# Two token tiles to a PSUM bank for the transposes of the exponentials and of the queries

## The chip, the cores and the metric

The kernel runs on one core of one Trainium2 chip, as one program. The metric is device time in microseconds from the first to the last instruction of one execution, with what the runtime adds around it. TensorE (PE) multiplies and transposes into PSUM; ScalarE (ACT) and VectorE (DVE) read PSUM and write SBUF; GpSimd (POOL) issues the gathers; SyncE (SP) issues the other transfers. Each engine runs its own stream in order, and the streams meet in semaphores.

## The reference, cut to what matters

A graph of 3125 nodes with 256 features and 100000 edges goes through one layer. Three things are added to the input: a graph convolution over the edges, four layers of linear attention with feed-forward blocks, and a mixture of 16 experts with two chosen per node. The change lies in the linear attention:

```python
def _linear_attn(x, Wq, Wk, Wv, Wo, bo):           # 8 heads of 32
    split = lambda t: t.reshape(b, n, HEADS, DH).transpose(0, 2, 1, 3)
    scale = DH ** (-0.25)
    q = jax.nn.softmax(split(x @ Wq) * scale, axis=-1)   # over a head's 32 columns
    k = jax.nn.softmax(split(x @ Wk) * scale, axis=-2)   # over all 3125 tokens
    v = split(x @ Wv)
    context = jnp.einsum('bhnd,bhne->bhde', k, v)
    out = jnp.einsum('bhnd,bhde->bhne', q, context)
    return out.transpose(0, 2, 1, 3).reshape(b, n, dm) @ Wo + bo

def _forward(x, ...):
    for i in range(4):
        x = x + _linear_attn(_layernorm(x, ln1_g[i], ln1_b[i]), ...)
        h = _layernorm(x, ln2_g[i], ln2_b[i])
        x = x + (jax.nn.gelu(h @ W1[i] + b1[i], approximate=False) @ W2[i] + b2[i])
    return x
```

## The kernel before, in words

**Tiles.** The 3125 tokens are 25 tiles of T = 125 tokens; five tiles (GT) are a group, and there are five groups (NG). 256 features are KD = 2 halves of 128. Pieces PC split a group in 3 and 2 tiles; units RP split it in 2, 1 and 2 tiles (NRP = 3 units).

**PSUM.** Eight banks of 512 fp32 columns. Two take edge products (`edge_bank`), one the sums over edges (`sum_bank`), two are the `ROW` pair that VectorE empties, and three (banks 4, 6, 7) are the ring, which ScalarE empties. Everything that TensorE puts into the ring is a numbered unit u; it goes to `RING[(u - RING_A) % 3]`. TensorE asks for a unit with `ring(u)` (line 1229), which waits until unit u - 3 has been copied out (`ring_act`), and reports it with `ring_full`. The numbers are laid out by hand in lines 348 to 406: `RING_GA` units per group in the key stage, `RING_MP` between, `RING_GP` per group in the feed-forward stage. The order in which TensorE fills units and ScalarE empties them must be the same.

**Key stage, per layer.** For each group g: TensorE waits until all earlier units are copied (line 1301), makes the keys, transposed, as four units (line 1310); VectorE takes the maximum over the tokens (1760) and from it a bias; ScalarE writes the exponentials `eT` (1012), features in partitions, tokens in columns. Meanwhile the next group's normalised tokens are transposed (1255) and scaled to `TT` or `TTQ` by ScalarE (`features`, 939). Then the exponentials are transposed back to tokens in partitions (1321 to 1327): one unit per token tile, two transposes of 128 columns each, and `copy_tile` (942 to 944, called at 1023 to 1025) copies each unit to `es[:, j, :]`, 125x256. The product of `es` with the normalised tokens is the context (`context`, 1287 to 1297), one group late; after the last group at once.

**Queries.** Query rows come from `Wq_s` through the `ROW` pair; VectorE and ScalarE make the softmax in `qe` (tokens in partitions). `queries_T` (TensorE 1266 to 1272, ScalarE 997 to 1000) transposes `qe` tile by tile: one unit per token tile, two transposes, one copy of 128x250 to `QT`. `attention(g, units)` (1277 to 1280) multiplies `QT` with `M_s`, unit by unit of RP, and waits at line 1279 until all tiles of the unit are copied. Group 0's queries are transposed between key and feed-forward stage, those of group g + 1 after the first half of the feed-forward block of group g (1380 to 1384).

**Edge steps.** The graph convolution's 224 edge steps are strewn by hand between all this (`step`): TensorE multiplies edge attributes (437) and sums rows by destination (429, 430), VectorE adds gathered rows (`z`, 477), ScalarE takes the positive part (`zr`, 445), VectorE the low part (`zl`, 451), GpSimd gathers the next rows (875). In ScalarE's stream an edge step stands right ahead of the copies of `es` in groups 0 to 3 (line 1022) and ahead of the copies of `QT` in groups 1 to 4 (line 1057); in the last key group the queries of group 0 stand there for TensorE (1318 to 1320).

**Graph stage, after the layers.** `pairs_T` (TensorE 1398 to 1405, ScalarE 1075 to 1080) already transposes by units of two, one and two tiles, with copies of 128x500 and 128x250.

Of the kernel before, what the change touches and what calls it, by code (L numbers as in the profile page):

```python
# [11 lines left out]
def build(nc, x, src, dst, edge_attr, gnn_W1, gnn_b1, gnn_W2,  # L12
# [56 lines left out]
    with ExitStack() as ctx:  # L69
# [12 lines left out]
        def sem(name):  # L82
# [235 lines left out]
        l_init, k_max, m_new, nb_done, cd_done, m_cp, corr_done = (sem(n) for n in (  # L318
            "l_init", "k_max", "m_new", "nb_done", "cd_done", "m_cp", "corr_done"))
# [29 lines left out]
        RING_GA = [4 + (LNU if g + 1 < NG else 0) + GT for g in range(NG)]  # L349
        RP = ((0, 2), (2, 3), (3, 5))  # L350
        NRP = len(RP)
        pair_of = lambda j: next(i for i, (a, b) in enumerate(RP) if a <= j < b)
        ROW_GA = 2
        RING_GP = [2 * NF + (GT + LNU if g + 1 < NG else 0) for g in range(NG)]
        QIN = [1 <= g < NG - 1 for g in range(NG)]
        ROW_GP = [NRP * (1 + (g + 1 < NG) + QIN[g]) for g in range(NG)]
        RING_MP, ROW_MP = 1 + GT + LNU, 3 * NRP + 1 + KD
# [46 lines left out]
        def ring_h2(l, g):  # L404
            return ring_qT(l, g) + GT
# [511 lines left out]
        def _(act):  # L917
# [56 lines left out]
            for l in range(L):  # L974
# [22 lines left out]
                def queries_T(g):  # L997
                    u = ring_qT(l, g)
                    for j in range(GT):
                        copy_tile(u + j, u + j - RING_A, QT[:, :, j * T:(j + 1) * T], T)  # L1000
# [5 lines left out]
                for g in range(NG):  # L1006
# [16 lines left out]
                    for j in range(GT):  # L1023
                        u = ring_k(l, g + 1) - GT + j
                        copy_tile(u, u - RING_A, es[:, j, :].rearrange("p (k n) -> p k n", k=KD), 128, T)
# [113 lines left out]
        def _(pe):  # L1139
# [119 lines left out]
            for l in range(L):  # L1259
# [6 lines left out]
                def queries_T(g):  # L1266
                    pe.wait_ge(q_norm, l * NG + g + 1)
                    for j in range(GT):
                        to = ring(ring_qT(l, g) + j)
                        for k in range(KD):  # L1270
                            ins = pe.transpose(to[:, 128 * k:128 * k + T], qe[:, j, 128 * k:128 * k + 128], ident[0:T, 0:T])
                        ins.then_inc(ring_full, 1)
# [4 lines left out]
                def attention(g, units):  # L1277
                    for i in units:
                        pe.wait_ge(ring_act, ring_qT(l, g) + RP[i][1] + 1)
                        rows_at(row_ao(l, g), i, lambda j: [(QT[:, k, j * T:(j + 1) * T], M_s[:, k, :]) for k in range(KD)])  # L1280
# [6 lines left out]
                def context(g):  # L1287
                    r0, uT = row_c(l, g), ring_k(l, g + 1) - GT
                    for pc, (a, b) in enumerate(PC):
                        to = row_of(r0 + pc)  # L1290
                        for h in range(KD):
                            for j in range(a, b):
                                if h == 0:
                                    pe.wait_ge(ring_act, uT + j + 2)
                                ins = pe.matmul(to[:, D * h:D * h + D], es[:, j, 128 * h:128 * h + 128], NORM[g % 2][:, j, :],  # L1295
                                                start=j == a, stop=j == b - 1)
                        ins.then_inc(row_full, 1)

                for g in range(NG):
                    u0, uT = ring_k(l, g), ring_k(l, g + 1) - GT  # L1300
# [20 lines left out]
                    for pc, (a, b) in enumerate(PC):  # L1321
                        for j in range(a, b):
                            pe.wait_ge(ring_act, u0 + (2 * pc + 3))
                            to = ring(uT + j)
                            for h in range(KD):
                                ins = pe.transpose(to[0:T, 128 * h:128 * h + 128], eT[:, h, j * T:(j + 1) * T], ident[:, :])
                            ins.then_inc(ring_full, 1)
# [715 lines left out]
```

## Time and profile before

| what | value |
|---|---|
| time, median of 3 runs | 2347.41 us (2334.14 to 2352.9) |
| the profiled execution: time | 2339.37 us |
| the profiled execution: span | 2337.6 us |
| mean granted TensorE clock | 0.935 of 2.4 GHz |
| busy: PE, PEld, DVE, ACT, POOL | 84%, 68%, 63%, 39%, 58% of the span |
| chain that ended last, by engine | PE 54%, DVE 18%, DMA 9%, ACT 7%, issue 6%, POOL 3% |

PE is TensorE's matrix work, PEld its weight loads, which overlap it. Busy time is a mean over stages with different limits; the chain is the work that released the next work, followed back from the last instruction, and tells which engine the end hung on at each moment. Its shares are of the whole span, the edge set-up before 180 us, four layers until about 1850 us, the graph stage and the experts included. Matmuls are pipelined, so the ends of PE pieces are modelled.

### The profile page before, as it was taken

The page shows a single profiled execution, that of the slowest core. Times are in us where ns is not written, and L with a number is a line of the kernel's source. Part 1 is how long each engine was busy: PE and PEld are TensorE (multiplying, and loading weights), DVE is VectorE, ACT ScalarE, POOL GpSimd, SP SyncE. Part 2 cuts the span into 40 slices and gives each one's busy share as a digit, 9 for nine tenths or more (in the row PEclk, how much of TensorE's full clock was granted, in tenths as well). Part 3 has the DMA queues.
Part 4 walks back from the last instruction along what each step waited for, and adds up shares of the span by engine and source line. Part 5 has one row for each costly group of instructions (what it writes and reads, how often), then busy time and mean ns, then how long its engine had stood idle before and what let it go on. Part 6 is the DMA issues. An engine that isn't in the chain of part 4 may idle for free.

```text
span 2337.6 us, 31898 instructions
## 1 busy us (share of the span) xinstructions
PE 1962.4 (84%) x10094; PEld 1594.8 (68%) x10094; DVE 1463.9 (63%) x3291; ACT 910.5 (39%) x1964; POOL 1356.0 (58%) x1123
## 2 busy tenths in 40 slices
PE   2448889999888999988899999889999985899990
PEld 1326667778666777866678777668777775788880
DVE  4747686766778677676876777686666557311116
ACT  1224344443435444344444444444444231233330
POOL 4157386667647666775666667567666500566650
PEclk9759999999999999999999999999999986899995
DMA  8564243333533332353333335343333421899997
GB/s 213 177 169 114 76 103 85 83 72 81 148 102 96 86 81 73 80 154 103 90 88 86 73 73 145 106 107 93 77 78 76 117 77 44 261 304 302 301 269 169
DMA packets 275536, 294.06 MB, mean 126 GB/s; under 512 B 146715, under 2 KB 204126, under 8 KB 275390
## 3 DMA queue, kind: packets, MB, share of 16 engines
q0 software_dynamic: 127488, 134.76, 24.0%
q1 hardware_dynamic: 143790, 157.50, 22.6%
q8 instruction: 70, 1.15, 0.2%
q10 hardware_dynamic: 4112, 0.03, 0.1%
q14 instruction: 76, 0.62, 0.1%
HBM read 243.19 MB, written 47.87 MB: 125 GB/s over the span
## 4 chain that ended last, share of the span: by engine, by line
PE 54%; DVE 18%; DMA 9%; ACT 7%; issue 6%; POOL 3%; SPq 1%; DVEq 1%; POOLq 0%; ACTq 0%
PE bank L1245 23%; PE bank L1373 11%; DMA TTQ<-zn_d,slot_tok 3%; PE bank L429 3%; PE bank L430 3%; PE bank L437 3%; DVE zl L451 2%; PE bank L1485 2%; DVE z L477 2%; DMA aT<-attr_d 2%; PE bank L1493 2%; ACT zr L445 2%; PE bank L1295 2%; POOL G L875 1%; PE bank L1310 1%
## 5 line engine op out<-in xcount | busy, mean ns | idle before, releaser
L875 POOL DMA_INDIRECT G<-P_d,src_T x896 | 1134.0, 1266 | 649.8 <-DVE z L477 382.6
L445 ACT ACTIVATE zr<-z 125x512 fp32r<-125x512 f32 x448 | 266.9, 629 | 349.2 <-DVE z L477 305.6
L451 DVE SCALAR_TENSOR_TENSOR zl<-z,zr 125x512 fp32r<-125x512 f32 x448 | 289.9, 688 | 140.3 <-ACT zr L445 130.9
L477 DVE TENSOR_TENSOR z<-bank,G 125x512 f32<-125x512 f32 x448 | 289.4, 684 | 136.7 <-PE bank L437 68.1
L1373 PE MATMUL bank<-TT,W_s 128*128 128x250 f32 (+1 forms) x1280 | 361.6, 428 | 15.9 <-ACT hid L1054 15.9
L1245 PE MATMUL bank<-W_s,hid 128*125 128x256 f32 x1600 | 361.1, 379 | 2.2 <-ACT hid L1054 2.2
L1245 PEld LDWEIGHTS bank<-W_s,hid 128*125 128x125 f32 x1600 | 293.8, 188 | 46.0 <-ACT hid L1054 3.8
L1373 PEld LDWEIGHTS bank<-TT,W_s 128*128 128x128 f32 x1280 | 235.7, 190 | 112.4 <-ACT hid L1054 23.1
L429 PE MATMUL bank<-zr,onehot 125*125 125x256 f32 x896 | 269.2, 332 | 21.8 <-DVE zl L451 21.7
L1054 ACT ACTIVATE hid<-bank,b_s 128x375 f32<-128x375 f32 x320 | 163.3, 521 | 271.3 <-PE bank L1373 223.6
L430 PE MATMUL bank<-zl,onehot 125*125 125x256 f32 x896 | 229.2, 286 | 0.0
L429 PEld LDWEIGHTS bank<-zr,onehot 125*125 125x125 f32 x896 | 170.9, 191 | 48.3 <-DVE onehot L464 30.1
L437 PE MATMUL bank<-Wst,aT 128*125 128x512 bf16 x448 | 139.2, 390 | 60.4 <-DMA aT<-attr_d 54.3
L430 PEld LDWEIGHTS bank<-zl,onehot 125*125 125x125 f32 x896 | 171.9, 192 | 5.6
L464 DVE TENSOR_TENSOR onehot<-iota_n,dst_T 125x500 fp32r<-125x500 f32 x224 | 152.5, 681 | 0.0
L1688 DVE TENSOR_TENSOR X<-bank,X 125x512 f32<-125x512 f32 (+1 forms) x120 | 71.5, 598 | 107.3 <-PE bank L1245 94.6
L437 PEld LDWEIGHTS bank<-Wst,aT 128*125 128x125 bf16 x448 | 59.4, 139 | 93.4 <-issue 49.4
L939 ACT ACTIVATE TT<-bank,lnp 128x250 f32<-128x250 f32 (+1 forms) x128 | 67.9, 613 | 114.8 <-PE bank L1255 109.9
L1119 ACT ACTIVATE QT<-bank,b1e 128x128 f32<-128x128 f32 x256 | 73.2, 369 | 98.8 <-PE bank L1485 76.3
L895 POOL DMA_INDIRECT TTQ<-zn_d,slot_tok x32 | 31.5, 986 | 137.9 <-DVE slot_tok L1971 121.3
L1245 PE MATMUL bank<-M_s,QT 128*125 128x256 f32 x400 | 104.9, 414 | 2.1 <-DVE M_s L1793 2.1
L1245 PE MATMUL bank<-Wq_s,TTQ 128*125 128x256 f32 x400 | 96.2, 381 | 5.8 <-DVE qe L1671 5.8
(317 smaller groups left out, 2953.1 us busy)
## 6 DMA issues: line engine op xcount, KB each, us to landing
W_s<-in_L_ffn_w SPq DMA_DIRECT2D x64, 512.0 KB
hid<-in_L_ffn_w SPq DMA_DIRECT2D x64, 512.0 KB
G<-P_d,src_T POOLq DMA_INDIRECT x896
TTQ<-nT_d SPq DMA_DIRECT2D x20, 626.0 KB
W_s<-in_L_mix_W SPq DMA_DIRECT2D x8, 1024.0 KB
nT_d<-TT SPq DMA_DIRECT2D x12, 626.0 KB
aT<-attr_d SPq DMA_DIRECT2D x224, 31.2 KB
nT_d<-TTQ SPq DMA_DIRECT2D x8, 626.0 KB
```

Source lines behind the costliest of these rows:

```text
L429: nc.tensor.matmul(sum_bank[0:T, 0:D], onehot[:, s, i, :], zr[:, s, i // 2, cols], start=i == 0, stop=False)
L430: ins = nc.tensor.matmul(sum_bank[0:T, 0:D], onehot[:, s, i, :], zl[:, i // 2, cols], start=False, stop=i == ST - 1)
L437: nc.tensor.matmul(edge_bank[k][0:ET, :], aT[:, s, :], Wst[:, 2 * k * D:2 * (k + 1) * D], start=True, stop=True).then_inc(e_done, 1)
L445: nc.scalar.activation(zr[:, s, k, :], z[:, k, :], ACT.Relu).then_inc(r_done, 1)
L451: nc.vector.scalar_tensor_tensor(zl[:, k, :], z[:, k, :], 0.0, zr[:, s, k, :].bitcast(f32), ALU.max, ALU.subtract).then_inc(lo_done, 1)
L464: nc.vector.tensor_tensor(onehot[:, s, :, :], iota_n[0:ET, :].unsqueeze(1).to_broadcast([ET, ST, T]), dst_T[:, ds(e * ST, ST)].unsqueeze(2 ...
L477: nc.vector.tensor_tensor(z[:, k, :], edge_bank[k][0:ET, :], G[:, ST * s + 2 * k:ST * s + 2 * k + 2, :].rearrange("p j d -> p (j d)"), ALU ...
L875: pool.indirect_dma_start(G[:, j, :], None, P_d[:, :], bass.IndirectOffsetOnAxis(ap=src_T[:, at:at + 1], axis=0)).then_inc(g_in[j], 16)
L1054: act.activation(hid[:, f, a * T:b * T], RING[(u - RING_A) % 3][:, 0:(b - a) * T], ACT.Gelu, bias=b1_s[:, l * NF + f:l * NF + f + 1]).then ...
L1119: ins = act.activation(hT[s % 2][:, c, :], RING[1 + s % 2][:, c * SL:(c + 1) * SL], ACT.Relu, bias=b1e[s][:, c:c + 1])
L1245: ins = pe.matmul(to[0:T, (j - a) * D:(j - a) * D + D], w, m, start=n == 0, stop=n == len(pairs) - 1)
L1373: ins = pe.matmul(to[:, 0:(b - a) * T], W1_s[:, k, part], TT[:, k, TT_PIECES[pc]], start=k == 0, stop=k == KD - 1)
```

## The change

Exponentials: the group's five tiles go into three units of RP instead of five; a unit of two tiles has four transposes, tile after tile, side by side in one bank, and one copy of 125x512 to `es[:, a:b, :]`; the middle one has two transposes and a copy of 125x256. Queries: the same, with the columns ordered by half and tile, and copies of 128x500, 128x250 and 128x500 to `QT`. The counts of ring units follow, and the waits of `context` and `attention` are moved to units. Two unused semaphores go.

```diff
-        RING_GA = [4 + (LNU if g + 1 < NG else 0) + GT for g in range(NG)]
+        RING_GA = [4 + (LNU if g + 1 < NG else 0) + NRP for g in range(NG)]
-        RING_GP = [2 * NF + (GT + LNU if g + 1 < NG else 0) for g in range(NG)]
+        RING_GP = [2 * NF + (NRP + LNU if g + 1 < NG else 0) for g in range(NG)]
-        RING_MP, ROW_MP = 1 + GT + LNU, 3 * NRP + 1 + KD
+        RING_MP, ROW_MP = 1 + NRP + LNU, 3 * NRP + 1 + KD
...
 ScalarE, queries_T(g)
-                    for j in range(GT):
-                        copy_tile(u + j, u + j - RING_A, QT[:, :, j * T:(j + 1) * T], T)
+                    for i, (a, b) in enumerate(RP):
+                        act.wait_ge(ring_full, u + i + 1)
+                        act.activation(QT[:, :, a * T:b * T], RING[(u + i - RING_A) % 3][:, 0:KD * (b - a) * T].rearrange("p (k n) -> p k n", k=KD),
+                                       ACT.Copy).then_inc(ring_act, 1)
...
 ScalarE, key stage
-                    for j in range(GT):
-                        u = ring_k(l, g + 1) - GT + j
-                        copy_tile(u, u - RING_A, es[:, j, :].rearrange("p (k n) -> p k n", k=KD), 128, T)
+                    for i, (a, b) in enumerate(RP):
+                        u = ring_k(l, g + 1) - NRP + i
+                        act.wait_ge(ring_full, u + 1)
+                        act.activation(es[:, a:b, :].rearrange("p j d -> p (j d)"), RING[(u - RING_A) % 3][0:T, 0:(b - a) * D],
+                                       ACT.Copy).then_inc(ring_act, 1)
...
 TensorE, queries_T(g)
-                    for j in range(GT):
-                        to = ring(ring_qT(l, g) + j)
+                    for i, (a, b) in enumerate(RP):
+                        to = ring(ring_qT(l, g) + i)
                         for k in range(KD):
-                            ins = pe.transpose(to[:, 128 * k:128 * k + T], qe[:, j, 128 * k:128 * k + 128], ident[0:T, 0:T])
+                            for j in range(a, b):
+                                at = (k * (b - a) + j - a) * T
+                                ins = pe.transpose(to[:, at:at + T], qe[:, j, 128 * k:128 * k + 128], ident[0:T, 0:T])
                         ins.then_inc(ring_full, 1)
...
 TensorE, attention(g, units)
-                        pe.wait_ge(ring_act, ring_qT(l, g) + RP[i][1] + 1)
+                        pe.wait_ge(ring_act, ring_qT(l, g) + i + 2)
...
 TensorE, context(g)
-                                    pe.wait_ge(ring_act, uT + j + 2)
+                                    pe.wait_ge(ring_act, uT + pair_of(j) + 2)
...
 TensorE, key stage
-                    for pc, (a, b) in enumerate(PC):
+                    for i, (a, b) in enumerate(RP):
+                        pe.wait_ge(ring_act, u0 + (3 if b <= PC[0][1] else 5))
+                        to = ring(uT + i)
                         for j in range(a, b):
-                            pe.wait_ge(ring_act, u0 + (2 * pc + 3))
-                            to = ring(uT + j)
                             for h in range(KD):
-                                ins = pe.transpose(to[0:T, 128 * h:128 * h + 128], eT[:, h, j * T:(j + 1) * T], ident[:, :])
-                            ins.then_inc(ring_full, 1)
+                                at = (j - a) * D + 128 * h
+                                ins = pe.transpose(to[0:T, at:at + 128], eT[:, h, j * T:(j + 1) * T], ident[:, :])
+                        ins.then_inc(ring_full, 1)
```

## Rows read from the trace of the kernel before

**Rows 1.** Source view of line 944: durations in ns (min/median/max), then who waited.

```profile
L944 ACT ACTIVATE es<-bank x100: 377/385/425, 190.6 to 1523.6; 125x256 f32<-125x256 f32 x100
...
  PEld bank L1271: 23.3, 19
...
  PEld bank L1326: 13.2, 16
...
  PEld bank L1310: 8.1, 12
```

**Rows 2.** Chain of waits in a key set: start us, us, what.

```profile
1047.60 1.04 ACT zr L445 x2
1048.64 0.28 ACT es L944
...
1049.06 0.47 PE bank L1326 x2
1049.55 0.67 ACT es L944 x2
1050.26 4.49 PE bank L1310 x8
```

**Rows 3.** Timeline of the same key set: start us, us, engine, line, operation [idle before].

```profile
1048.51 1.70 ACT L944 ACTIVATE es<-bank 125x256 f32<-125x256 f32 x5
...
1046.84 1.35 PE L1326 MATMUL bank<-ident,eT 128*125 128x128 f32 x6 [0.22 <-ACT TT L939]
```

**Rows 4.** Chain of waits in a query set.

```profile
872.18 1.23 ACT zr L445 x2
873.41 0.28 ACT QT L944
873.73 0.70 PE bank L1271 x4
```

**Rows 5.** Timeline of the same query set, ScalarE and TensorE.

```profile
873.32 1.54 ACT L944 ACTIVATE QT<-bank 128x250 f32<-128x250 f32 x5
878.77 1.23 ACT L445 ACTIVATE zr<-z 125x512 fp32r<-125x512 f32 x2 [3.92 <-DVE z L477]
...
871.60 0.86 PE L1271 MATMUL bank<-ident,qe 125*128 125x125 f32 x6 [0.49 <-DVE qe L1681]
...
874.27 2.76 PE L1245 MATMUL bank<-M_s,QT 128*125 128x256 f32 x12
```

**Rows 6.** Source view of line 1079, the copies of the graph stage.

```profile
L1079 ACT ACTIVATE QT<-bank x15: 373/588/597, 1844.7 to 1922.4; 128x500 f32<-128x500 f32 x10, 128x250 f32<-128x250 f32 x5
```

**Rows 7.** Timeline of ScalarE in the graph stage.

```profile
1844.74 1.34 ACT L1079 ACTIVATE QT<-bank 128x500 f32<-128x500 f32 x3 [2.83 <-PE bank L1404]
```

**Rows 8.** Timeline of ScalarE behind the first key set of layer 2.

```profile
1028.92 1.28 ACT L930 ACT_TABLE_LOAD   x1
```

**Rows 9.** Timeline of VectorE behind the first key set of layer 0.

```profile
195.64 0.69 DVE L477 TENSOR_TENSOR z<-bank,G 125x512 f32<-125x512 f32 x1 [2.24 <-DMA G<-P_d,src_T]
```

**Rows 10.** Chain of waits in a first query set.

```profile
1118.04 0.86 PE bank L1271 x6
1118.90 0.04 issue
1118.94 0.70 PE bank L1271 x4
```

**Rows 11.** Timeline of TensorE behind a last key set.

```profile
1108.13 4.58 PE L1295 MATMUL bank<-hn,es 125*128 125x256 f32 x20 [0.34 <-DVE qe L1671]
```

**Rows 12.** Stretches of query and key sets: us, busy of five engines, PEclk, DMA, GB/s.

```profile
392.89:400.09 7.20, 5.90 (x24) 4.63 (x25) 4.01 (x8) 2.72 (x8) 5.02 (x4) 0.76 0.21 46
...
1642.50:1649.70 7.20, 5.91 (x25) 4.68 (x25) 4.03 (x8) 2.84 (x8) 5.02 (x4) 0.76 0.18 50
...
227.73:234.93 7.20, 5.84 (x17) 3.61 (x18) 2.39 (x4) 3.30 (x9) 4.31 (x4) 0.78 0.57 163
...
1480.88:1488.08 7.20, 5.85 (x17) 3.54 (x18) 2.32 (x4) 3.30 (x9) 4.30 (x4) 0.76 0.59 166
```

**Rows 13.** Timeline of ScalarE in a query set with the lower clock.

```profile
810.88 1.53 ACT L944 ACTIVATE QT<-bank 128x250 f32<-128x250 f32 x5
818.02 1.23 ACT L445 ACTIVATE zr<-z 125x512 fp32r<-125x512 f32 x2 [5.61 <-DVE z L477]
```

More of the change, by code:

```diff
@@ L317, in build @@
         b_stat, b_aggr, b_std, b_rstd = (sem(n) for n in ("b_stat", "b_aggr", "b_std", "b_rstd"))
-        l_init, k_max, m_new, nb_done, cd_done, m_cp, corr_done = (sem(n) for n in (
-            "l_init", "k_max", "m_new", "nb_done", "cd_done", "m_cp", "corr_done"))
+        l_init, k_max, nb_done, cd_done, corr_done = (sem(n) for n in (
+            "l_init", "k_max", "nb_done", "cd_done", "corr_done"))
         cn_done, rk_done, key_summed = sem("cn_done"), sem("rk_done"), sem("key_summed")
@@ L404, in ring_h2 @@
         def ring_h2(l, g):
-            return ring_qT(l, g) + GT
+            return ring_qT(l, g) + NRP
         def row_c(l, g):
@@ L1287, in context @@
                 def context(g):
-                    r0, uT = row_c(l, g), ring_k(l, g + 1) - GT
+                    r0, uT = row_c(l, g), ring_k(l, g + 1) - NRP
                     for pc, (a, b) in enumerate(PC):
@@ L1299, in _ @@
                 for g in range(NG):
-                    u0, uT = ring_k(l, g), ring_k(l, g + 1) - GT
+                    u0, uT = ring_k(l, g), ring_k(l, g + 1) - NRP
                     pe.wait_ge(ring_act, u0 + 1)
```

## The prediction

> **What bounds the kernel now.** I read the chain of waits first, then the source view of the copies (line 944), then timelines of one stretch of each kind. No single engine is the limit in these stretches; the end is set by a relay from engine to engine, and the sets of transposes and copies are links of it. The source view says how much TensorE waits for the copies at all: its weight loads sat idle 23.3 us before the query transposes, 13.2 us before the transposes of the exponentials and 8.1 us before the key products that come next [rows 1]. These 44.6 us in 47 waits are the most that the two edits can take off TensorE directly.
>
> There are 40 sets, 20 of exponentials and 20 of queries, of five kinds. The reader should see what holds each.
>
> *Key sets of groups 1 to 3 (12).* The chain runs from the two `zr` activations of an edge step, which end at 1048.64, into the first `es` copy, from there into two transposes, back into two copies, and then into the key products at 1050.26 [rows 2]. So six transposes go out while ScalarE is still on `zr`; the fourth unit of the ring needs the first copy, TensorE stands still, and the last two copies come behind the late transposes. The five copies run from 1048.51 for 1.70 us [rows 3].
>
> *Query sets of groups 1 to 4 (16).* The same picture: `zr`, 0.28 us of the first `QT` copy, then the last four transposes for 0.70 us on the chain [rows 4]. TensorE sent six transposes, waited, and its attention products start at 874.27, right behind the last transposes, because the copies they need are long done [rows 5].
>
> *First key set of layers 1 to 3 (3), first key set of layer 0 (1), last key sets (4), first query sets (4)*: below.
>
> **The price of one copy.** The old kernel has the wide form already, in the graph stage: a copy of 128x500 takes 588 ns at the median [rows 6], and a run of 500, 250 and 500 columns takes 1.34 us in all [rows 7]; the one-tile copy takes 385 ns [rows 1]. That a wide copy would cost as much as two narrow ones is ruled out by these rows.
>
> **The change part by part.**
>
> *Key sets, 12.* Transposes: three units fit into the three banks, so none waits for a copy of its own set. The first six are still held by the features before them (0.22 us on `TT`, then 1.35 us for six) [rows 3]; four more at the rate of the six cost 0.9 us at most, so the last unit is full by 1049.1. ScalarE starts where it starts now (it comes from `zr`), at 1048.51, and takes 1.34 us scaled by 512/500 in the wide copies, some 1.36 us: it ends at 1049.87 instead of 1050.21. The third copy starts about 0.75 us into the run, 1049.26, after its unit is full. The key products follow 0.05 us later as now. Gain 0.34 us each, 12 x 0.34 = 4.1 us. Nothing else ends last there: the chain goes from the copies to the products directly [rows 2].
>
> *Query sets, 16.* Ten transposes without a wait take 10/6 of the 0.86 us that six take [rows 5], 1.43 us from 871.60, done at 873.03. Now attention has to wait for the first copy, which holds two tiles. That copy starts at 873.32 as before (after `zr`), takes 0.588 us, and TensorE restarts after a copy's end in about 0.16 us (1048.51 + 0.385 to the transposes' 1049.06 [rows 1 to 3]): 874.07 instead of 874.27. Gain 0.20 us, 16 x 0.20 = 3.2 us. What is late next is this first copy itself. The second copy, one tile, is done some 0.65 us after the first; the first unit's four products out of the twelve that take 2.76 us last 0.9 us [rows 5], so no second wait.
>
> *First key set, layers 1 to 3.* Behind the copies ScalarE loads a table at 1028.92 for the deviations on which VectorE's edge step waits [rows 8]: 0.34 us earlier, 3 x 0.34 = 1.0 us. In layer 0 the edge step waits 2.24 us for gathered rows [rows 9], so the gain there is lost and I count nothing.
>
> *First query sets, 4.* Ten transposes on the chain take 1.60 us in all, six of them 0.86 [rows 10]; at that rate ten take 1.43. Gain 0.17, 4 x 0.17 = 0.7 us.
>
> *Last key sets, 4.* The context products behind them wait 0.34 us for VectorE's `qe` [rows 11], not for copies: nothing. If that cover were gone, the wider last copy would cost 0.588 - 0.385 = 0.20 us in these four and the four first query sets, the places where ScalarE is free before the transposes are done: 1.6 us.
>
> *Added wait.* A wide copy waits for four transposes instead of two. Behind it on ScalarE stand the other copies of the set, nothing else; in the 32 sets with an edge step's `zr` ahead of the copies ScalarE comes late and the wait is over. No DMA is issued or moved, and SyncE's and GpSimd's queues wait on counts that lie ahead of these units. The dropped semaphores are used by nobody.
>
> *Eighty fewer copies* as such are not on the path except as counted.
>
> Sum of the waits: 4.1 + 3.2 + 1.0 + 0.7 = 9.0 us, between a loss of 1.6 us (all absorbed, the cover gone) and the 44.6 us of all waits for copies.
>
> The Trainium skill, "ScalarE: Activation LUTs", section "What ACT_TABLE_LOAD costs", speaks against part of this: an activation with immediate scale and bias costs 186 ns plus 0.833 ns per column, but back-to-back ones overlap by some 93 ns, so most of a merged copy's fixed cost was hidden already. By it the three copies take about 1.44 us (an estimate from that page) and a key set gains 0.26 instead of 0.34, the whole sum about 1.2 us less. The rows of the graph stage say 1.34 us, and a row decides.
>
> **The clock.** TensorE's granted clock falls from 2.4 to 1.2 GHz for a while behind some of these sets: 7 of the 16 query stretches (the first and last of the seven are shown) and 5 of the 12 key stretches show a mean below 1 [rows 12]. The price of one is read between two equal sets: from the first copy to the next `zr` it is 818.02 - 810.88 = 7.14 us with the fall and 878.77 - 873.32 = 5.45 us without [rows 5, 13], 1.69 us. What the change does to it no row of before shows; the ends are all twelve lifted (12 x 1.69 = 20.3 us gained) and the other sixteen sets falling too (27.0 us lost). What stands before each fall is a TensorE that idled between transposes and products. In the query set that idle goes from 873.73 - (871.60 + 0.86) = 1.27 us before the last four transposes [rows 4, 5] to 874.07 - 873.03 = 1.04 us, a sixth less; in the key set, between the sixth transpose's end at 1048.19 and the products and less four transposes of 0.143 us, from 1.50 to 1.16 us, a quarter less. In proportion that is one of the seven and one of the five: two falls, 3.4 us.
>
> Total: 9.0 + 3.4 = 12.4 us. The profiled execution took 2339.4 us (2337.6 of span), so on its own time 2327; the median of the runs shown is 8.0 us above it, and I take the same off the median: 2347.4 - 12.4 = **2335 us**.
>
> **The rivals.**
>
> *The clock gives more back* (faster by over 1%). If no TensorE idle in these sets leads to a fall any more, all twelve go: 9.0 + 20.3 = 29.3 us, 2318 us. For it: falls are seen behind fewer than half of sets that look alike, so they stand near an edge, and the change makes every idle a little shorter. Against: ScalarE still comes late from `zr`, and one idle of over a microsecond remains. The Trainium skill, "TensorE: Matmul & The Clock Gate", section "A second HAM failure mode: psum-queue depth-cycling", describes this: TensorE that idles briefly between groups while it cycles through PSUM banks has its clock taken down and up again; the rows here agree that the falls follow such idles.
>
> *The gain is absorbed* (no change). What comes next waits for something that has its own time, as in layer 0's first set the gathered rows [rows 9]. Then 2347 us, within 3 us. For it: one set does just that. Against: in the other kinds the chain passes from the copies straight on to TensorE work [rows 2, 4].
>
> *The one long idle pulls the clock down* (slower). Place: behind the key and query sets that keep 2.4 GHz today. The idle in a key set is now in two pieces, 1049.06 - (1046.84 + 1.35) = 0.87 us before the late transposes and then the wait for the last copy [rows 2, 3]; afterwards it is one piece. If one piece of 1.0 to 1.2 us decides, the other sixteen fall too: 27.0 - 9.0 = 18.0 us lost, 2365 us. It becomes a loss from six added falls on (6 x 1.69 = 10.1 against 9.0). Against: total idle does not grow in either kind.
>
> **How the numbers follow.** Chances: forecast 0.52, clock gives back most 0.18, absorbed 0.23, clock pulled down 0.07. The forecast's own range is 2324 to 2343 (one to six falls lifted or two added, and the spread of the runs). The range goes from the first rival, 2318 less a margin of 1, to the upper end of the runs before with nothing gained, 2353; the last rival and the tail under 2318 are left out, about 1.5 in 10. About 1%, 23 us, is what a measurement can tell from no change here. Faster by more: the first rival and a thin edge of the forecast that falls beyond 2324, 0.20. Slower by more needs 23 us, beyond the sixteen falls: 0.03. The rest, 0.77, is within 1%.
>
> **What would show it.** In the profile after: the wait of query and exponential transposes for a copy (23.3 and 13.2 us) gone; a new wait of the attention products for `QT`, about 1 us in 16 places; three copies of a key set in some 1.36 us, and the key products some 3.0 us after the set's first transpose instead of 3.4; the first key set of layer 0 no shorter in what follows. The count of stretches below 2.4 GHz says which clock case holds. The forecast is wrong if the copies run slower than 1.34 us in a row, if the products that follow start no earlier, or if the number of falls moves by more than six either way.

## The result, and the profile after

The changed kernel takes 2318.1 us at the median (2310.2 to 2328.9). The kernel before took 2337.2 us at the median of eight runs, the three shown ahead of the prediction and five more beside the changed kernel; that is some 10 us less than the median of the three. The ratio is 0.9919, interval 0.9899 to 0.9940: 19 us less, between 14 and 24. The profiled execution has a span of 2319.8 us against 2337.6, so 17.8 us less, and the readings below are made on that.

The page of the changed kernel: busy time and share of each engine with its instructions, the chain that ended last, and the attention products.

```profile
PE 1948.4 (84%) x10094; PEld 1591.0 (69%) x10094; DVE 1464.0 (63%) x3291; ACT 900.8 (39%) x1884; POOL 1356.6 (58%) x1123
...
PE 56%; DVE 16%; DMA 11%; ACT 7%; issue 4%; POOL 3%; SPq 2%; DVEq 1%; POOLq 0%; ACTq 0%
...
L1249 PE MATMUL bank<-M_s,QT 128*125 128x256 f32 x400 | 98.1, 393 | 16.1 <-ACT QT L1001 14.0
```

ScalarE has 80 instructions fewer and was busy 9.7 us less (910.5 before). The attention products wait 14.0 us for `QT`, for which they did not wait before.

**The copies, and who waits for them.** Source view of the changed kernel: the copies of the exponentials (L1028) and of the queries (L1001), with durations in ns (min/median/max) and who waited, in us and times.

```profile
L1028 ACT ACTIVATE es<-bank x60: 377/598/639, 192.8 to 1510.5; 125x512 f32<-125x512 f32 x40, 125x256 f32<-125x256 f32 x20
...
  PEld bank L1316: 19.3, 12
  PE bank L1316: 16.8, 12
...
L1001 ACT ACTIVATE QT<-bank x60: 371/570/601, 284.5 to 1753.2; 128x500 f32<-128x500 f32 x40, 128x250 f32<-128x250 f32 x20
...
  PEld bank L1249: 18.4, 16
  PE bank L1249: 14.0, 16
```

Against [rows 1]: the 23.3 us before the query transposes (now L1277) and the 13.2 us before the transposes of the exponentials (now L1333) are gone. The idle time stands in other places: 18.4 us before the attention products' loads, in all 16 query sets, and 19.3 instead of 8.1 us before the key products' loads, in the same 12 sets as before. Most of the 44.6 us was moved, since ScalarE comes as late as it did.

**A key set.** The chain of waits of the changed kernel (start us, us, what):

```profile
1041.20 1.03 ACT zr L445 x2
1042.23 1.26 ACT es L1028 x3
1043.49 0.04 issue
1043.54 2.80 PE bank L1316 x8
```

Its timeline (start us, us, engine, line, operation, idle before):

```profile
1040.44 1.57 PE L1333 MATMUL bank<-ident,eT 128*125 128x128 f32 x10 [0.22 <-ACT TT L939]
...
1042.10 1.38 ACT L1028 ACTIVATE es<-bank 125x512 f32<-125x512 f32 x3
...
1043.54 2.79 PE L1316 MATMUL bank<-TT,Wk_s 128*128 128x375 f32 x8 [1.52 <-ACT es L1028]
```

Where [rows 2, 3] go from ScalarE to TensorE and back, this chain goes over once. Ten transposes run together in 1.57 us, the three copies take 1.38 us (five: 1.70), and the products start 1043.54 - 1040.44 = 3.10 us after the first transpose. Before it was 1050.26 - 1046.84 = 3.42 [rows 3], and TensorE's rows in between were:

```profile
1049.06 0.73 PE L1326 MATMUL bank<-ident,eT 128*125 128x128 f32 x4 [0.86 <-ACT es L944]
1050.26 4.48 PE L1310 MATMUL bank<-TT,Wk_s 128*128 128x375 f32 x8 [0.47 <-ACT es L944]
```

So TensorE stood still 0.86 + 0.47 = 1.33 us before and 1.52 us after, in one piece: the set became shorter and its idle longer.

**A query set.** The chain and then the timeline of the changed kernel.

```profile
451.87 1.23 ACT zr L445 x2
453.10 0.48 ACT QT L1001
453.58 0.04 issue
453.63 2.85 PE bank L1249 x12
```

```profile
451.29 1.29 PE L1277 MATMUL bank<-ident,qe 125*128 125x125 f32 x10 [0.49 <-DVE qe L1688]
...
453.01 1.32 ACT L1001 ACTIVATE QT<-bank 128x500 f32<-128x500 f32 x3
...
453.63 2.85 PE L1249 MATMUL bank<-M_s,QT 128*125 128x256 f32 x12 [1.05 <-ACT QT L1001]
...
458.23 1.23 ACT L445 ACTIVATE zr<-z 125x512 fp32r<-125x512 f32 x2 [3.91 <-DVE z L477]
```

The last transposes have left the chain [rows 4], and one wide copy has taken their place; TensorE idles 1.05 us for it. The products start 453.63 - 451.29 = 2.34 us after the first transpose, where it was 874.27 - 871.60 = 2.67 [rows 5], and take 2.85 us instead of 2.76. From the first transpose to the next `zr` the set takes 458.23 - 451.29 = 6.94 us; before, 878.77 - 871.60 = 7.17 [rows 5].

**The clock.** A query set with a fall, cut in two stretches, transposes and products: us, busy time of PE, PEld, DVE, ACT and POOL with instructions, the granted clock, DMA share, GB/s. First a set of the kernel before, then one of the changed kernel.

```profile
516.10:518.60 2.50, 1.20 (x9) 0.91 (x10) 2.50 (x5) 1.94 (x6) 1.33 (x2) 0.99 0.00 0
518.60:523.30 4.70, 4.70 (x17) 3.77 (x17) 1.53 (x4) 0.90 (x3) 3.69 (x3) 0.64 0.31 69
```

```profile
509.00:511.83 2.83, 1.12 (x5) 0.69 (x5) 2.76 (x4) 2.44 (x5) 0.00 (x0) 1.00 0.09 34
511.83:514.13 2.30, 1.92 (x10) 1.53 (x10) 2.30 (x5) 1.74 (x5) 1.21 (x1) 0.60 0.00 0
514.13:519.03 4.90, 4.87 (x23) 4.17 (x24) 2.87 (x7) 0.73 (x2) 3.81 (x3) 0.84 0.30 72
```

Before, the transposes ran at full speed and the low clock (0.64 over the stretch) lay on the attention products. After, it begins with the transposes (0.60) and is over earlier in the products (0.84). The timeline of that set says what this costs:

```profile
511.82 1.93 PE L1277 MATMUL bank<-ident,qe 125*128 125x125 f32 x10 [0.49 <-DVE qe L1688]
...
513.54 1.32 ACT L1001 ACTIVATE QT<-bank 128x500 f32<-128x500 f32 x3
...
514.16 3.61 PE L1249 MATMUL bank<-M_s,QT 128*125 128x256 f32 x12 [0.41 <-ACT QT L1001]
...
519.51 0.63 ACT L445 ACTIVATE zr<-z 125x512 fp32r<-125x512 f32 x1 [4.66 <-DVE z L477]
```

The transposes take 1.93 instead of 1.29 us, but TensorE waits for the copy anyway: its idle shrinks from 1.05 to 0.41 us and the products start 2.34 us behind the first transpose, as in the set without a fall. Only the products lose time. The set takes 519.51 - 511.82 = 7.69 us, 0.75 more than 6.94; a fall in the kernel before cost 1.69 [rows 5, 13].

### The profile page after: what moved, and what is told of

Read it like the earlier page. It is cut to its first block, busy times and chain, and to the rows that moved or that the text cites. A ratio compares the mean times of both kernels' runs of the same rounds, so it can differ in the third digit from the quotient of the medians.

```text
span 2319.8 us, 31778 instructions
## 1 busy us (share of the span) xinstructions
PE 1948.4 (84%) x10094; PEld 1591.0 (69%) x10094; DVE 1464.0 (63%) x3291; ACT 900.8 (39%) x1884; POOL 1356.6 (58%) x1123
## 4 chain that ended last, share of the span: by engine, by line
PE 56%; DVE 16%; DMA 11%; ACT 7%; issue 4%; POOL 3%; SPq 2%; DVEq 1%; POOLq 0%; ACTq 0%
PE bank L1249 24%; PE bank L1380 11%; DMA aT<-attr_d 4%; PE bank L429 3%; PE bank L430 3%; DMA TTQ<-zn_d,slot_tok 3%; PE bank L437 3%; PE bank L1492 3%; PE bank L1500 2%; POOL G L875 2%; PE bank L1301 2%; ACT zr L445 2%; DVE z L477 2%; DMA G<-P_d,src_T 2%; PE bank L1316 2%
## 5 line engine op out<-in xcount | busy, mean ns | idle before, releaser
L429 PE MATMUL bank<-zr,onehot 125*125 125x256 f32 x896 | 270.9, 334 | 21.5 <-DVE zl L451 21.4
L1695 DVE TENSOR_TENSOR X<-bank,X 125x512 f32<-125x512 f32 (+1 forms) x120 | 71.5, 599 | 94.4 <-PE bank L1249 94.4
L1249 PE MATMUL bank<-M_s,QT 128*125 128x256 f32 x400 | 98.1, 393 | 16.1 <-ACT QT L1001 14.0
```

Source lines behind the costliest of these rows:

```text
L429: nc.tensor.matmul(sum_bank[0:T, 0:D], onehot[:, s, i, :], zr[:, s, i // 2, cols], start=i == 0, stop=False)
L1249: ins = pe.matmul(to[0:T, (j - a) * D:(j - a) * D + D], w, m, start=n == 0, stop=n == len(pairs) - 1)
```

## The experiments

Each kernel was timed in five rounds beside the kernel before; a ratio is to that kernel.

**One part alone (e1, e2).** The changed kernel with the queries, or the exponentials, put back. The core of e1, then of e2:

```diff
 ScalarE, queries_T(g)
-                    for i, (a, b) in enumerate(RP):
-                        act.wait_ge(ring_full, u + i + 1)
...
+                    for j in range(GT):
+                        copy_tile(u + j, u + j - RING_A, QT[:, :, j * T:(j + 1) * T], T)
```

```diff
 ScalarE, key stage
-                    for i, (a, b) in enumerate(RP):
-                        u = ring_k(l, g + 1) - NRP + i
...
+                    for j in range(GT):
+                        u = ring_k(l, g + 1) - GT + j
+                        copy_tile(u, u - RING_A, es[:, j, :].rearrange("p (k n) -> p k n", k=KD), 128, T)
```

> Only the exponentials lie two tiles to a bank; queries as before. If the gain is the waits for copies: twelve key sets 0.32 us shorter and three first key sets, 4 to 5 us less than before, ratio 0.998. If it is mostly the clock: the key sets behind which the clock falls (5 of 12 before) go to 2 or fewer and the gain is 8 us or more, ratio 0.996 or lower.

> Only the queries lie two tiles to a bank; exponentials as before. Waits: sixteen query sets 0.23 us shorter and four first sets 0.3 us, 5 us less, ratio 0.998. Clock: a fall behind a query set costs 0.75 us where it cost 1.69 and there are fewer, 8 to 10 us more, together 13 to 15 us, ratio 0.994. Waits and clock of both halves should add up to the whole change's 19 us (0.992).

e1 took 2326.2 us, ratio 0.9944 (0.9923 to 0.9965); e2 2325.8, 0.9952 (0.9933 to 0.9972). Each part gives about half. Added up the two gains are 1.04%, where both parts together gave 0.81 (and 0.97 when they were timed again, e9 below), which the intervals allow. In e1's profile the falls of the clock (counted as in [rows 12]) in the key sets go from five to three. In e2's the sixteen query sets are as short as in the changed kernel (114.58 us in sum against 114.24, from 127.08), but seven key sets have a fall where five had one, though nothing was changed there.

**Wide units, narrow copies (e3).** Three units as in the changed kernel, but five copies.

```diff
-                        act.activation(es[:, a:b, :].rearrange("p j d -> p (j d)"), RING[(u - RING_A) % 3][0:T, 0:(b - a) * D],
-                                       ACT.Copy).then_inc(ring_act, 1)
+                        for j in range(a, b):
+                            ins = act.activation(es[:, j, :], RING[(u - RING_A) % 3][0:T, (j - a) * D:(j - a + 1) * D], ACT.Copy)
+                        ins.then_inc(ring_act, 1)
...
```

> Three units as after, but ScalarE copies each tile by itself (five narrow copies, one signal a unit). If the units are the cause (no transpose waits for a copy of its own set): the key products and the attention start 0.06 us later than after, 28 x 0.06 = 2 us given back, so 17 us less than before, ratio 0.993. If the fewer copies are the cause: back to the time of before, ratio 0.999 to 1.0.

2326.3 us, ratio 0.9954 (0.9936 to 0.9972), about half the gain. Its timeline of a key set:

```profile
1059.52 1.57 PE L1337 MATMUL bank<-ident,eT 128*125 128x128 f32 x10 [0.21 <-ACT TTQ L939]
...
1061.18 1.49 ACT L1032 ACTIVATE es<-bank 125x256 f32<-125x256 f32 x5
...
1062.72 2.79 PE L1320 MATMUL bank<-TTQ,Wk_s 128*128 128x375 f32 x8 [1.64 <-ACT es L1032]
```

Five copies without a wait among them take 1.49 us, so of the 1.70 of before 0.2 was the wait for the ring and 0.1 the narrow form. By these waits e3 should lose 12 x 0.12 + 16 x 0.06 = 2.4 us against the changed kernel. By the middles of the ratios it lost about 8; what makes the rest stays open (the two intervals overlap). In the profiled execution the sets of e3 are 4.5 us longer than the changed kernel's, so 2.1 us beyond the waits, with six query falls instead of four.

**The clock without the waits (e5, e4).** e5 is the kernel before with the third tile's transposes repeated in the time in which TensorE would stand still; e4 is the changed kernel with the last unit's repeated. The repeats write the same values again. First e5, then e4.

```diff
 TensorE, queries_T(g)
-                        for k in range(KD):
+                        for k in list(range(KD)) * (5 if g and j == 2 else 1):
...
 TensorE, key stage
-                            for h in range(KD):
+                            for h in list(range(KD)) * (3 if g + 1 < NG and j == 2 else 1):
```

```diff
 TensorE, queries_T(g)
-                        for k in range(KD):
+                        for k in list(range(KD)) * (3 if g and i == NRP - 1 else 1):
...
 TensorE, key stage
-                        for j in range(a, b):
+                        for j in list(range(a, b)) * (2 if g + 1 < NG and i == NRP - 1 else 1):
```

> The kernel before, with the third tile's transposes repeated (8 more in a query set of groups 1 to 4, 4 more in a key set of groups 0 to 3) while TensorE would wait for the first copy; same values to the same place. The waits stay. If the falls of the clock hang on TensorE's idle in these sets: fewer than 12 falls behind them and up to 20 us less, ratio 0.992 to 0.996. If only the waits count: 0 to 1 us, ratio 1.000.

> The changed kernel with the last unit's transposes repeated (8 more in a query set of groups 1 to 4, 4 more in a key set of groups 0 to 3), same values to the same place, while TensorE would wait for the first copies. Waits as after. If falls hang on TensorE's idle in these sets and a fall still costs 0.7 (queries) to 1.7 us (keys): none to three falls where the profiles of after show four to eight, 3 to 8 us less than after, ratio to before 0.988 to 0.990. If what is left of the falls has another cause: as after, 0.991.

e5: 2326.8 us, ratio 0.9950 (0.9934 to 0.9966), so 11.7 us from useless work. A query set without a fall takes 7.17 us as before, so no wait became shorter. Eleven falls are left of twelve (6 query, 5 key), but one of a query set costs 0.96 us in the mean of six (0.95 in the one shown, 8.12 - 7.17). Timeline of such a set in e5:

```profile
863.73 3.61 PE L1271 MATMUL bank<-ident,qe 125*128 125x125 f32 x18 [0.49 <-DVE qe L1681]
...
867.13 3.00 PE L1245 MATMUL bank<-M_s,QT 128*125 128x256 f32 x12
```

The stretch of the repeated transposes, 863.73 to 867.13, has a granted clock of 0.57, and the products behind it run nearly at full rate (3.00 us against 2.76): the useless work takes the low clock upon itself. That a gain of this size can be had with every wait left as it was is shown; its 11.7 us is more than the query falls explain (7 x 1.69 - 6 x 0.96 = 6.1), and the rest is not settled.

e4: 2319.0 us, 0.9919 (0.9891 to 0.9947), no faster than the changed kernel, though its falls go from eight to two. Its profile says where the gain went: the 28 sets are 8.1 us shorter in sum than the changed kernel's, but the first key and query sets of the layers are 2.9 us longer, and the four times from the fourth to the fifth key set are 5.8 us longer, 95.1 us against 89.3. What holds those is shown under e12.

**The order of ScalarE's work (e10, e6, e7, e8).** The edge step's `zr` stands ahead of the copies in ScalarE's stream. e10 is the kernel before, five narrow copies, with the query copies moved ahead of `zr`. e6 is the changed kernel with the first two query copies ahead; e7 has the key copies ahead; e8 has both. First e10, then e6, then e7.

```diff
-                        if f - 1 in FF_STEP:
+                        if f - 1 in FF_STEP and (f < NF - 1 or g + 1 == NG):
                             step(e0 + FF_STEP[f - 1])
...
                         queries_T(g + 1)
+                        step(e0 + 3)
```

```diff
-                        if f - 1 in FF_STEP:
+                        if f - 1 in FF_STEP and (f < NF - 1 or g + 1 == NG):
...
-                        queries_T(g + 1)
+                        queries_T(g + 1, (0, 1))
+                        step(e0 + 3)
+                        queries_T(g + 1, (2,))
```

```diff
-                        step(step_k(l, g) + 1)
                     for i, (a, b) in enumerate(RP):
...
+                    if g + 1 < NG:
+                        step(step_k(l, g) + 1)
```

> The kernel before (five units, five narrow copies), with ScalarE's five query copies ahead of the edge step's zr instead of behind it in 16 places. If the ring is short only because ScalarE comes late: the fourth unit's wait falls from 1.27 us to under 0.3, attention starts 1.0 us earlier, 16 us and most of the falls behind the query sets, 8 us more: ratio 0.990. If five units in three banks hold TensorE by themselves: less than 5 us, ratio 0.998.

> After, with ScalarE's first two query copies ahead of the edge step's zr instead of behind it (16 places). If TensorE's attention is held by ScalarE coming late from zr: it starts about 1.4 us after the set's first transpose instead of 2.34, 0.9 x 16 = 14 us less than after, so 33 us less than before, ratio 0.986. If zr, now 0.9 us later, holds VectorE's zl and the residual behind it: nothing gained over after, ratio 0.992, and a wait of zl for zr of up to 1 us more a set.

> After, with the es copies ahead of the edge step's zr in key groups 0 to 3 (16 places). If the copies are held by zr: the key products start about 2.25 us after the set's first transpose instead of 3.09, 0.85 x 12 = 10 us less than after, 29 us less than before, ratio 0.988. If VectorE's zl, later by 1.4 us, then ends after the key products: nothing gained, ratio 0.992.

> Both moves together. If both are independent links of the chain: 14 + 10 us less than after, 43 us less than before, ratio 0.982. If the edge steps take over as the bound: 0.988 to 0.992.

| kernel | us | ratio | interval |
|---|---|---|---|
| e10 | 2315.8 | 0.9909 | 0.9887 to 0.9932 |
| e6 | 2301.7 | 0.9824 | 0.9799 to 0.9850 |
| e7 | 2325.8 | 0.9920 | 0.9895 to 0.9944 |
| e8 | 2304.4 | 0.9836 | 0.9811 to 0.9861 |

Timeline of a query set in e10:

```profile
860.65 1.60 PE L1272 MATMUL bank<-ident,qe 125*128 125x125 f32 x10 [0.49 <-DVE qe L1682]
861.12 1.55 ACT L944 ACTIVATE QT<-bank 128x250 f32<-128x250 f32 x5 [0.45 <-PE bank L1272]
...
862.09 2.76 PE L1246 MATMUL bank<-M_s,QT 128*125 128x256 f32 x12
862.56 1.14 ACT L445 ACTIVATE zr<-z 125x512 fp32r<-125x512 f32 x2
```

With five units on three banks and narrow copies TensorE no longer stands still, and the products start 862.09 - 860.65 = 1.44 us after the first transpose; the change as made needs 2.34. In the query sets the ring was too short only because ScalarE came late. One query fall is left of seven, while the falls in key sets go from five to seven. This reorder alone gives as much as the change under study.

Timeline of a query set in e6:

```profile
858.90 1.29 PE L1280 MATMUL bank<-ident,qe 125*128 125x125 f32 x10 [0.49 <-DVE qe L1691]
859.59 0.86 ACT L1002 ACTIVATE QT<-bank 128x500 f32<-128x500 f32 x2 [0.67 <-PE bank L1280]
860.23 2.85 PE L1252 MATMUL bank<-M_s,QT 128*125 128x256 f32 x12
```

1.33 us from first transpose to products. The set takes 5.93 us instead of 6.94, up to the start of the next step's `zr` at 864.83, and 16 of them give 16 us of the 18 to 22 by which e6 beats the changed kernel (18 against e9, timed beside it, 22 against the first measurement).

e7 gained nothing over the changed kernel, and e8 nothing over e6. Its key sets start sooner after each other (16.9 us instead of 17.38 in the middle of a layer), but the last group's edge step comes to wait. Timeline of e7 there:

```profile
1495.74 1.29 DVE L451 SCALAR_TENSOR_TENSOR zl<-z,zr 125x512 fp32r<-125x512 f32 x2 [2.29 <-ACT zr L445]
...
1501.73 1.11 PE L437 MATMUL bank<-Wst,aT 128*125 128x512 bf16 x2 [3.69 <-DMA aT<-attr_d]
```

VectorE waits 2.29 us for the `zr` that was moved back, and TensorE 3.69 us for attribute rows. That second wait is where a part of the changed kernel's gain goes too, and the next pair takes it away.

**The transfer that absorbs (e12, e11).** In the key loop SyncE issues the write and read of the normalised tokens ahead of the next group's attribute rows. The waits for these rows by TensorE's loads, in the layers (us in total, times, longest us), in the kernel before, in the changed kernel and in e7:

```profile
PEld bank L437 <- DMA aT<-attr_d: 17.4, 11, 4.1
```

```profile
PEld bank L437 <- DMA aT<-attr_d: 24.1, 13, 4.4
```

```profile
PEld bank L437 <- DMA aT<-attr_d: 37.8, 14, 5.8
```

Each gain in the key sets lengthens this wait: e1, which changes them alone, has 24.1 us as well, e2, which leaves them, 17.2, and e8 39.5. Timeline of the changed kernel in a last key group, SyncE's issues and TensorE:

```profile
1488.25 0.33 SPq L712 DMA_DIRECT2D nT_d<-TT  x1
1488.67 0.38 SPq L715 DMA_DIRECT2D TTQ<-nT_d  x1
1489.10 16.97 SPq L507 DMA_DIRECT2D aT<-attr_d  x4
...
1490.56 2.79 PE L1316 MATMUL bank<-TT,Wk_s 128*128 128x375 f32 x8 [1.52 <-ACT es L1028]
...
1495.95 0.65 PE L437 MATMUL bank<-Wst,aT 128*125 128x512 bf16 x2 [2.61 <-DMA aT<-attr_d]
```

The rows are issued 0.85 us behind a write and 0.43 us behind a read of 626 KB each, and are used 6.85 us after their issue, 2.61 of it as a wait; over the whole kernel such rows land 2.9 us after their issue at the median. e12 is the changed kernel with the first of these rows issued one turn earlier; e11 is e8 with the same.

```diff
-                    attr_steps(at, step_k(l, g + 1))
-                    at = max(at, step_k(l, g + 1))
+                    to = step_k(l, g + 1) + (1 if g + 1 < NG else 0)
+                    attr_steps(at, to)
+                    at = max(at, to)
```

> After, with SyncE issuing the attribute rows of the next group's first edge step ahead of the write of the normalised tokens (key groups 0 to 3) instead of behind it and the reload. If the key sets' gain in groups 0 and 3 went into the wait for these rows: TensorE's 24 us of that wait falls below 8 us, and the kernel takes 8 to 16 us less than after, ratio to before 0.985 to 0.988. If the rows were not the bound there: as after, 0.991.

> After, with both sets of copies ahead of zr and the attribute rows issued early. Against the move of the query copies alone (0.982): if the key copies' move was lost to the wait for the rows, now some 8 x 0.5 us of the middle groups and 8 to 16 us of groups 0 and 3 come back: ratio 0.975 to 0.978. If not: 0.982.

> The changed kernel again, on the chip of the three others, for comparison: 0.990 to 0.994 of before. Waits of copies as in its first profile; the number of stretches with a lower clock behind the 28 sets, 8 in the first profile, is expected to differ by two or three from execution to execution if it depends on where the sets happen to fall.

e12: 2299.3 us, 0.9846 (0.9821 to 0.9871). e11: 2277.5 us, 0.9755 (0.9731 to 0.9778), the best kernel of the study, by the ratios 35 to 38 us faster than the changed one (against e9 and against the first measurement). The waits in e12:

```profile
PEld bank L437 <- DMA aT<-attr_d: 6.7, 3, 2.9
```

The time from the fourth to the fifth key set goes from 21.6 to 22.9 us in the changed kernel to 18.8 in three layers and 20.7 in layer 0. So the gain of these groups was there and was taken by the transfer. e9, the changed kernel again, gave 2319.8 us, 0.9903 (0.9877 to 0.9930), which agrees with the first measurement. Its profiled execution has falls in 3 query and 1 key stretches where the first one has 4 and 4. Its 28 sets are 6.6 us shorter in sum, yet its span is 2321.3 us against 2319.8, and the four times from the fourth to the fifth key set take 94.4 us instead of 89.3: here, as in e4, most of what fewer falls gave went into the wait for the attribute rows.

## Why the prediction was right, and where its sizes were off

The forecast was 12.4 us less; 19 (14 to 24) were measured, 17.8 in the profiled span. The table takes every set from its first transpose to ScalarE's next link (the correction's exponential, the table load or the next `zr`), summed over the sets of a kind in the two profiled executions. The waits are the difference between sets at full clock; the clock is what is left. All in us.

| sets | before | after | gain | of it waits | waits forecast | of it clock |
|---|---|---|---|---|---|---|
| key, groups 1 to 3 (12) | 95.61 | 89.65 | 5.96 | 12 x 0.32 = 3.8 | 4.1 | 2.1 |
| query, groups 1 to 4 (16) | 127.08 | 114.24 | 12.84 | 16 x 0.23 = 3.7 | 3.2 | 9.1 |
| first key (4) | 14.63 | 13.70 | 0.93 | 0.9 | 1.0 | |
| first query (4) | 16.60 | 14.91 | 1.69 | 4 x 0.32 = 1.3 | 0.7 | 0.4 |
| sum | 253.9 | 232.5 | 21.4 | 9.7 | 9.0 | 11.7 |

The starts of the transposes tell what of it arrived. From the first key set of each layer to its first query set, 3.7 us of the 6.9 that the key sets gained show up; from there to the next layer, or to the last query set, 13.5 us of the 14.5 of the query sets. So the key stage absorbed 3.2 us. The rest of the 17.8 us in the span is the difference of two stretches that the change does not touch: 2.2 us more ahead of the first key set, 2.7 less from the last query set to the end.

**The waits: right.** Three copies of a key set were to take 1.36 us and took 1.38; the key products were to follow 3.0 us after the first transpose and follow after 3.10. The Trainium skill, "ScalarE: Activation LUTs", section "What ACT_TABLE_LOAD costs", gave an estimate of 1.44 us for the run of three; the trace has 1.38 for it, nearer to the 1.34 of the graph stage [rows 7]. By the letter this 1.38 meets a sign that the forecast had named against itself (slower than 1.34 us in a row); the run of `QT`, which has the graph stage's widths, takes 1.32. In the query sets the new wait appeared in all 16 places at 1.05 us, and the gain was 0.23 instead of 0.20. Two errors nearly cancel in this: the products start 0.33 us earlier, not 0.20, since they follow the first copy with 0.04 us on the chain, not 0.16; and they then take 0.09 us longer, which was not counted. In the first query sets the ten transposes on the chain take 1.29 us, not the 1.43 scaled from six, so they alone give 1.60 - 1.29 = 0.31 us; their copies are not on the chain, in either kernel, where the products behind them wait 0.52 us for VectorE's `M_s`.

**Layer 0's first set: right.** Its copies take 1.42 instead of 1.68 us, and VectorE then waits longer for the gathered rows, 2.50 us against 2.24 [rows 9]:

```profile
197.96 0.69 DVE L477 TENSOR_TENSOR z<-bank,G 125x512 f32<-125x512 f32 x1 [2.50 <-DMA G<-P_d,src_T]
```

**What absorbs: the rival named the right kind and not the place.** That a later wait would take gains was given to gathered rows. It happens, for a part, at the attribute rows in the key stage: the changed kernel waits 24.1 - 17.4 = 6.7 us longer for them. In layer 2 one such wait falls on the time from the first to the second key set, 24.5 us against 21.3, and the four times from the first to the second key set grow by 2.9 us in sum although every first set became shorter. e12 shows the cause: with the rows issued earlier the wait goes to 6.7 us in all, and the kernel gains 13 to 17 us more (0.9846 against 0.9903 of e9 and 0.9919).

**The clock: the term that was mis-sized.** Here the forecast took a fixed price of 1.69 us for a fall and two falls fewer, 3.4 us. The runs showed two other things. The number went from 7 and 5 to 4 and 4, four fewer (3 and 1 in e9). And the price in a query set went from 1.69 to a mean of 0.72 us (7.60 to 7.69 in the four sets, against 6.94): the fall now begins with the transposes, whose slowness is hidden by the wait for ScalarE. In the query sets the seven falls before cost 12.3 us together (six 1.67 to 1.69, one 2.21) and the four after 2.9; that is 9.4 us, and 9.1 stand in the table because one set without a fall was held up in each kernel. The rest of the clock term lies mostly in the key sets, where a fall still costs 1.63 to 1.99. How firm the two parts are is seen where other executions run the same code: the sums of the query sets agree within 1.4 us (114.24 and 112.87 in the changed kernel and e9, 127.08 and 126.35 in the kernel before and e1); those of the key sets are 5 us apart (89.65 and 84.40, and 95.61 against 100.81 in e2). So the 9.1 us are clear of this, the 2.1 are not. e5 moves the falls in the same way without the change, and there the price is 0.96.

The step of the argument that failed is "what stands before each fall is a TensorE that idled between transposes and products". In the changed kernel the clock is down with the set's first transposes, before that idle. What stands ahead of it is the stretch at the end of the feed-forward part, where TensorE was busy 1.12 of 2.83 us (509.00 on, above); but the set without a fall shown above has the same stretch ahead of it (1.12 of 2.80 us from 448.50 on), so this does not decide alone. Nor did the idle change as the proportion assumed: in the key sets it was to go from 1.50 to 1.16 us and went from 1.33 to 1.52, and yet these falls did not grow in number. So a proportion of the idle inside the set could tell neither number nor price. The Trainium skill, "TensorE: Matmul & The Clock Gate", section "A second HAM failure mode: psum-queue depth-cycling", puts the cost down to throttling and warming between bursts; these traces add that what it costs depends on which work lies under it.

**The rivals.** The measured time is the number of the rival in which all falls go, 2318 us, but by chance: eight falls are left, and the forecast was set against a median 10 us above that of all eight runs. Of the 17 us between the 2335 us that were forecast and the 2318.1 measured, 10 come from this and 7 from the change itself. It is luck as well that the time lies inside the stated range, 1 us above its lower end of 2317; the forecast's own part of it, 2324 to 2343, missed. The rival with a longer idle that pulls the clock down is excluded: the idle before the products did become one piece, of 1.05 us in the query sets and 1.52 in the key sets, and the falls became fewer.

**What stays open.** Most of the 5 to 6 us that e3 seems to lose beyond its waits, the half of e5's gain that the query falls don't explain, and why one of several equal sets has a fall and the next has none. Nor was the best kernel taken apart: the gains of the changed kernel, e6 and e12 alone add up to 0.81 + 0.95 + 0.73 = 2.49%, and e11 has 2.45%, so what the key copies ahead of `zr` add in it isn't shown.

## What to carry to other kernels

Before you make a buffer larger because an engine waits for it, look at what the engine that empties it was doing: here it stood in another step's work, and moving its copies ahead of that step gave with the small units as much as the larger units did. Price a fall of the clock by the work that lies under it, hidden or on the chain, not by a constant. When a gain in one group comes back as a wait for a small transfer, look at what is queued ahead of it; issuing it one turn earlier was worth 13 to 17 us here, against 19 to 23 for the change itself.

## What the runs showed of the hardware

Repeating transposes that nobody needs, in time in which TensorE would otherwise wait, made the kernel before 11.7 us faster (e5): the work itself did no harm, and in the query sets it carried the low clock in place of the products.

The mean granted clock of a whole span is no measure here. It went from 0.935 to 0.927 while the time fell by 17.8 us. That difference lies in the edge set-up, which the change does not touch: 0.77 and 0.68 over the first 180 us. From 180 to 1850 us, where the layers are, it was 0.97 before and 0.98 after. So the clock of a stretch has to be read in that stretch.

A run of narrow copies costs ScalarE little more than the wide ones: five of 125x256 in 1.49 us (e3) against three of up to 125x512 in 1.38 us, although one alone takes 385 ns [rows 1] and a wide one 598.
